# Reordering one turn of a woven attention pipeline: four steps change place in a hand-written order

## The chip, the cores and the metric

The kernel runs on one core of a Trainium2 chip. The metric is the device time of one launch in microseconds (us). Three executions of the kernel before took 490.29, 494.37 and 494.52 us, with a median of 494.37 us. A fourth one, the profiled execution, took 486.01 us.

## What is computed

Sixteen sequences of 256 rows and 128 columns go through three residual blocks. Everything is float32 at the interface.

```python
x = x + 0.5 * ffn(layernorm(x))      # gate, up, silu(gate)*up, down; inputs and weights rounded to FP4 in blocks of 16
x = x + attention(layernorm(x))      # 16 heads of 8, causal, softmax, output projection and bias
x = x + 0.5 * ffn(layernorm(x))
```

In the attention, scores are Q K^T / sqrt(8), masked below the diagonal, softmax over the keys, times V, then `Y @ Wo + bo`.

## The kernel before, in words

The kernel is written engine by engine: every engine has its own program, and semaphores tie them together. One batch is one sequence. The work on a batch is cut into named steps, and `ATT_LAG` says how many turns behind the newest batch a step works, so that in one turn each step works on another batch. A turn is one pass over `ATT_ORDER`. Each engine walks that same list and issues only its own part of each step, in the list's order. Inside an engine nothing overtakes: what stands behind a waiting instruction waits with it. So the list sets, for every engine at once, what is queued behind what.

Turns 0 to 4 of the attention are woven into the end of the first feed-forward block. Turns 5 to 7 run the full list, turns 8 to 15 are a loop of four turns, turns 16 to 19 again run the full list (with a few feed-forward steps between), and turns 20 to 22 use other lists. Turn 5 is the first with exponentials (ST0 to ST4), turn 7 the first with an output projection, turn 16 the last with a query-key projection. Turns 7 to 16 therefore hold both projections: ten turns. The norm's apply step ends with turn 16 too.

The steps that matter here, with their lines:

- `S0` to `S11`: TensorE computes scores (L1268), VectorE takes the row maximum of each (L1050). They use the PSUM banks s0, s1, s2 in turn.
- `nmS`: VectorE splits the maxima into three bf16 parts. `nm`: TensorE transposes them (L1278), ScalarE copies them out (L779, `nmT`), and a DMA issued by SyncE (L506) writes them into rows of `q_stack`.
- `ST0` to `ST11`: TensorE computes transposed scores, with the maxima subtracted through those rows (L1299), ScalarE takes the exponential (L790), GpSimd masks (L619). They use the banks st0 and st1 in turn, so TensorE's part of one waits for ScalarE's exponential of the one two before it. `ST0` also waits for the DMA of `nm`. In a turn the order is ST5 to ST11 of one batch, then ST0 to ST4 of the next.
- `AV0` to `AV3`: value products (L1326, L1330). `oc0`, `oc1`: ScalarE copies them out (L800). `oT0`, `oT1`: TensorE transposes them (L1341). `n0`, `n1`: VectorE divides by the row sums (L1073, L1075). `oT1` needs the bank that `n0` frees.
- `yT`: TensorE transposes the result (L1349). `yTc`: ScalarE copies it (L809). `wo`: TensorE's output projection (L1356), whose stationary operand is that copy. `wa`: VectorE adds it to x (L1083).
- `lnN`: ScalarE applies the norm to the next batch (L661). `xT`: TensorE transposes it (L1236). `xTc`: ScalarE copies it (L754). `qk`: TensorE's query and key projections (L1245). `c1`: ScalarE's first bf16 part of them (L760). `split`: VectorE's remainder (L1041). `c2`: the second part (L764).

Waits are placed by helpers such as this one of TensorE, which waits until the last user of the step's bank has been read:

```python
def bank_for(step, b, it):
    user = bank_user_before(step, it, NB)
    if user:
        k, n = count(*user)
        pe.wait_ge(taken[k], n)
...
def wo(b, s, it):
    ps, done = bank_for("wo", b, it)
    pe.wait_ge(taken["yT"], b + 1)
```

Of the kernel before, what the change touches and what calls it, by code (L numbers as in the profile page):

```python
# [82 lines left out]
    "oT0 oT1 n0 n1 yT yTc wo wa sS sA sE",  # L83
)) for step in steps.split()}
ATT_ORDER = """
nmS ST5 S0 oT0 third  ST6 lnN n0 S1  ST7 nm S2 stack  ST8 S3 AV0 AV1 bias
ST9 oc0 oT1 xT n1 S4  ST10 xTc lnS S5  ST11 lnA S6 yT  ST0 yTc lnE S7 qk wo
ST1 c1 wa S8  ST2 split S9 AV2 AV3  ST3 c2 oc1 sS S10 v  ST4 sA S11 sE
""".split()
ATT_UNROLL = 4  # L90
PART_TURNS = 2
# [1300 lines left out]
```

## Time and profile before

| what | value |
|---|---|
| profiled execution, device time | 486.01 us |
| span of its instructions | 484.3 us |
| outside the span | 1.7 us |
| TensorE matmul busy | 387.2 us (80%) |
| TensorE weight load busy | 283.9 us (59%) |
| VectorE busy | 425.9 us (88%) |
| ScalarE busy | 318.3 us (66%) |
| GpSimd busy | 258.1 us (53%) |
| mean granted TensorE clock | 0.979 of 2.4 GHz |
| median of three other executions | 494.37 us |

The busy shares are means over stages that differ. The first feed-forward block fills the span up to about 145 us, the attention with full turns runs from about 158 to 347 us, and the second feed-forward block ends at 484.3 us. The change touches only the middle part, so that part has to be read by itself, and there by the order in which waits end, since no engine's share alone says which one sets the pace. In the rows below, PE is TensorE, PEld its weight loads, DVE is VectorE, ACT is ScalarE, POOL is GpSimd.

### The profile page before, as it was taken

What the parts mean: (1) busy time and instruction counts of PE and PEld (TensorE: products, weight loads), DVE (VectorE), ACT (ScalarE), POOL (GpSimd) and SP (SyncE); (2) the same over time, 40 slices, a digit from 0 to 9 for tenths busy, and PEclk for the clock granted to TensorE, in tenths of its full rate; (3) what the DMA queues carried; (4) which work ended last, traced back from release to release, by engine and by line L of the source; (5) the groups of instructions that cost most, each with busy time, mean ns of one, the idle gap of its engine ahead of it and who ended that gap; (6) DMA issues with size and microseconds to landing.
All of it is one profiled execution on the core that took longest, in us unless ns stands there. A gap on an engine that the chain in (4) does not pass through costs nothing.

```text
span 484.3 us, 12396 instructions
## 1 busy us (share of the span) xinstructions
PE 387.2 (80%) x3433; PEld 283.9 (59%) x3433; DVE 425.9 (88%) x1132; ACT 318.3 (66%) x861; POOL 258.1 (53%) x479
## 2 busy tenths in 40 slices
PE   0557877878786799999999999988795777887786
PEld 0334656656574577777666767666553556665665
DVE  3787999998988989888888898888869989999994
ACT  3566788868752677777777787766763646656642
POOL 6464656645525466777777777555661243233321
PEclk9997999989999899999999999999998989999999
DMA  7887000000545454444445544450000000000001
GB/s 221 236 133 124 2 1 0 1 1 0 146 143 143 133 143 135 135 131 135 127 137 145 145 134 129 131 147 4 3 1 1 2 22 21 13 22 22 22 18 37
DMA packets 38440, 39.30 MB, mean 81 GB/s; under 512 B 1789, under 2 KB 35453, under 8 KB 36093
## 3 DMA queue, kind: packets, MB, share of 16 engines
q1 hardware_dynamic: 38397, 38.79, 30.3%
q8 instruction: 20, 0.33, 0.3%
q14 instruction: 23, 0.19, 0.1%
HBM read 21.91 MB, written 10.49 MB: 67 GB/s over the span
## 4 chain that ended last, share of the span: by engine, by line
PE 36%; issue 26%; ACT 11%; DVE 10%; POOL 8%; DMA 7%; ACTq 1%; POOLq 1%; SPq 0%; DVEq 0%
DMA q_stack<-nmT 6%; PE bank L1299 6%; PE bank L1326 5%; PE bank L1159 5%; PE bank L1160 4%; PE bank L1268 3%; ACT probs L790 3%; POOL hq_out L551 3%; PE bank L1188 2%; PE bank L1245 2%; PE bank L1356 2%; PE bank L1330 2%; POOL xq_out L551 2%; PE bank L1146 2%; POOL fln_rstd L577 1%
## 5 line engine op out<-in xcount | busy, mean ns | idle before, releaser
L790 ACT ACTIVATE probs<-bank 128x512 f32<-128x512 f32 x192 | 111.3, 603 | 48.3 <-PE bank L1299 47.2
L1050 DVE TENSOR_REDUCE nm<-bank 128x2 f32<-128x512 f32 (+1 forms) x192 | 125.9, 680 | 6.0 <-PE bank L1268 5.7
L619 POOL TENSOR_SCALAR_AFFINE_SELECT probs<-probs 128x256 f32<-128x256 f32 (+1 forms) x192 | 90.1, 485 | 62.5 <-ACT probs L790 61.0
L1299 PE MATMUL bank<-q_stack,k_stack 75*128 75x256 bf16 (+1 forms) x512 | 73.4, 247 | 9.9 <-ACT probs L790 5.5
L1268 PE MATMUL bank<-k_stack,q_stack 127*128 127x256 bf16 (+1 forms) x512 | 74.0, 249 | 1.5 <-DVE nm L1050 1.5
L551 POOL TENSOR_TENSOR xq_out<-xq_grid,xq_scale 128x256 f32<-128x256 bf16 x32 | 24.4, 762 | 83.5 <-DVE xq_grid L894 83.5
L1159 PE MATMUL bank<-wguT,f_xT 128*128 128x352 f32 x128 | 56.9, 529 | 6.7 <-ACT f_xT L713 4.5
L720 ACT ACTIVATE f_silu<-bank 128x352 f32<-128x352 f32 x64 | 29.6, 463 | 46.8 <-PE bank L1160 45.9
L1188 PE MATMUL bank<-wdT,f_hT 128*128 128x128 f32 (+1 forms) x384 | 53.4, 275 | 1.4 <-ACT f_hT L731 1.4
L1188 PEld LDWEIGHTS bank<-wdT,f_hT 128*128 128x128 f32 (+1 forms) x384 | 49.9, 191 | 6.5 <-issue 0.9
L1299 PEld LDWEIGHTS bank<-q_stack,k_stack 75*128 75x128 bf16 x512 | 37.1, 97 | 27.4 <-ACT probs L790 13.7
L1160 PE MATMUL bank<-wguT,f_xT 128*128 128x352 f32 x128 | 53.0, 499 | 0.0
L551 POOL TENSOR_TENSOR hq_out<-hq_grid,hq_scale 128x704 f32<-128x704 bf16 x31 | 42.8, 1380 | 11.7 <-DVE hq_grid L894 11.7
L1146 PE MATMUL bank<-ident,xq_out 128*128 128x128 f32 x64 | 14.2, 305 | 42.8 <-POOL xq_out L551 28.1
L1268 PEld LDWEIGHTS bank<-k_stack,q_stack 127*128 127x128 bf16 x512 | 40.8, 99 | 7.5 <-DVE nm L1050 3.1
L1326 PE MATMUL bank<-probs,v_stack 128*32 128x256 f32 x512 | 40.2, 386 | 0.2 <-DVE oT L1090 0.2
L1146 PEld LDWEIGHTS bank<-ident,xq_out 128*128 128x128 f32 x64 | 6.7, 144 | 51.2 <-POOL xq_out L551 31.8
L1015 DVE TENSOR_TENSOR f_h<-f_silu,bank 128x352 f32<-128x352 f32 x64 | 30.9, 515 | 6.4 <-ACT f_silu L720 6.1
L1160 PEld LDWEIGHTS bank<-wguT,f_xT 128*128 128x128 f32 x128 | 26.6, 208 | 15.9 <-issue 4.0
L1159 PEld LDWEIGHTS bank<-wguT,f_xT 128*128 128x128 f32 x128 | 23.3, 208 | 21.1 <-ACT f_xT L713 14.6
L1179 PE MATMUL bank<-ident,hq_out 128*128 128x128 f32 (+1 forms) x192 | 32.0, 276 | 4.0 <-ACT f_hT L731 3.6
L713 ACT COPY f_xT<-bank 128x256 f32<-128x256 f32 x31 | 11.5, 371 | 25.9 <-PE bank L1146 25.9
(149 smaller groups left out, 894.4 us busy)
## 6 DMA issues: line engine op xcount, KB each, us to landing
q_stack<-q_parts SPq DMA_DIRECT2D x16, 576.0 KB
k_stack<-k_parts SPq DMA_DIRECT2D x16, 576.0 KB
q_parts<-qk_parts SPq DMA_DIRECT2D x16, 192.0 KB, 2.1
k_parts<-qk_parts SPq DMA_DIRECT2D x16, 192.0 KB, 2.4
v_stack<-zeros_bf SPq DMA_DIRECT2D x1, 2048.0 KB, 10.2
k_parts<-qk_parts SPq DMA_DIRECT2D x16, 128.0 KB, 2.3
out_dram<-x_all SPq DMA_DIRECT2D x15, 128.0 KB, 1.8
q_stack<-mask_q SPq DMA_DIRECT2D x1, 1664.0 KB
```

The source lines that it names most:

```text
L551: nc.gpsimd.tensor_tensor(q.out[:, s, :].rearrange("p (n k) -> p n k", k=BLOCK), q.grid[:, s, :].rearrange("p (n k) -> p n k", k=BLOCK), q ...
L619: nc.gpsimd.affine_select(out=v, in_=v, compare_op=ALU.is_ge, fill=0.0, base=0, pattern=[[0, heads], [1, P]], channel_multiplier=-1).then_ ...
L790: nc.scalar.activation(probs[:, c, :], ps[:, :], ACT.Exp, scale=SCALE).then_inc(done, 1)
L1015: nc.vector.tensor_tensor(f_h[:, j, :], f_silu[:, j, :], ps.up[j][:, 0:I], ALU.mult).then_inc(h_ready[j], 1)
L1050: nc.vector.tensor_reduce(nm[:, j, h0:h0 + n], ps[:, :].rearrange("p (h k) -> p h k", h=n), AX_X, ALU.max, negate=True).then_inc(done, 1)
L1159: nc.tensor.matmul(ps.gate[j][:, 0:I], x, wguT[:, 0, :], start=True, stop=True)
L1160: nc.tensor.matmul(ps.up[j][:, 0:I], x, wguT[:, 1, :], start=True, stop=True).then_inc(gu_filled[j], 1)
L1179: last = nc.tensor.transpose(ps.hT[0:k, P * t:P * t + P], hquant.out[:, s, I * j + P * t:I * j + P * t + k], ident[:, :])
L1188: nc.tensor.matmul(out, f_hT[0:k, t, P * j:P * j + P], wdT[0:k, t, :], start=(t == 0), stop=False)
L1268: last = nc.tensor.matmul(ps[:, keys * h:keys * h + keys], q_stack[0:ROWS, s, h0 + h, P * j:P * j + P], k_stack[0:ROWS, s, h0 + h, 0:keys] ...
L1299: last = nc.tensor.matmul(ps[:, w * n:w * n + w], k_stack[0:SROWS, s, HG * g + h, k0:k0 + P], q_stack[0:SROWS, s, HG * g + h, q0:T], start ...
L1326: nc.tensor.matmul(ps[VW * h:VW * h + VW, 0:T], window(s, 0, h), probs[:, slot + h // 2, T * (h % 2):T * (h % 2) + T], start=(half == 0), ...
```

## The change

Only the list of one turn changes.

```diff
 ATT_ORDER = """
-nmS ST5 S0 oT0 third  ST6 lnN n0 S1  ST7 nm S2 stack  ST8 S3 AV0 AV1 bias
-ST9 oc0 oT1 xT n1 S4  ST10 xTc lnS S5  ST11 lnA S6 yT  ST0 yTc lnE S7 qk wo
-ST1 c1 wa S8  ST2 split S9 AV2 AV3  ST3 c2 oc1 sS S10 v  ST4 sA S11 sE
+nmS ST5 S0 oT0 third  ST6 n0 S1  ST7 nm lnN S2 stack  ST8 S3 oT1 n1 AV0 AV1 bias
+ST9 oc0 xT S4  ST10 xTc lnS S5  ST11 lnA S6 yT  ST0 yTc lnE S7 wo qk c1
+ST1 wa S8  ST2 split S9 AV2 AV3  ST3 c2 oc1 sS S10 v  ST4 sA S11 sE
 """.split()
```

No instruction is added or removed. VectorE, GpSimd and SyncE keep their orders: `n1` stays between S3 and S4 on VectorE, since the value products issue nothing there. TensorE and ScalarE change.

On TensorE, the end of a full turn's first half, before (S3 is the first row; L1326 and L1330 are AV0 and AV1, L1299 is ST9, L1341 is oT1, L1236 is xT):

```order
256 L1268 MATMUL bank<-k_stack,q_stack 128x128 x4
257 L1326 MATMUL bank<-probs,v_stack 32x256 x4
258 L1330 MATMUL bank<-probs,v_stack 32x128 x4
259 L1326 MATMUL bank<-probs,v_stack 32x256 x4
260 L1330 MATMUL bank<-probs,v_stack 32x128 x4
261 L1299 MATMUL bank<-q_stack,k_stack 128x256 x2
262 L1341 MATMUL bank<-ident,oT 128x128 x2
263 L1236 MATMUL bank<-ident,aln_out 128x128 x2
```

The same place now:

```order
256 L1268 MATMUL bank<-k_stack,q_stack 128x128 x4
257 L1341 MATMUL bank<-ident,oT 128x128 x2
258 L1326 MATMUL bank<-probs,v_stack 32x256 x4
259 L1330 MATMUL bank<-probs,v_stack 32x128 x4
260 L1326 MATMUL bank<-probs,v_stack 32x256 x4
261 L1330 MATMUL bank<-probs,v_stack 32x128 x4
262 L1299 MATMUL bank<-q_stack,k_stack 128x256 x2
263 L1236 MATMUL bank<-ident,aln_out 128x128 x2
```

The second output transpose has moved ahead of AV0, AV1 and ST9.

On TensorE, later in the same turn, before (the rows are yT, ST0, S7, qk, wo, ST1, S8):

```order
269 L1349 MATMUL bank<-ident,y 128x128 x2
270 L1299 MATMUL bank<-q_stack,k_stack 128x256 x2
271 L1268 MATMUL bank<-k_stack,q_stack 128x256 x2
272 L1245 MATMUL bank<-a_xT,wqk 128x256 x2
273 L1356 MATMUL bank<-wqkvo,yT 128x128 x2
274 L1299 MATMUL bank<-q_stack,k_stack 128x256 x2
275 L1268 MATMUL bank<-k_stack,q_stack 128x256 x2
```

The same place now:

```order
269 L1349 MATMUL bank<-ident,y 128x128 x2
270 L1299 MATMUL bank<-q_stack,k_stack 128x256 x2
271 L1268 MATMUL bank<-k_stack,q_stack 128x256 x2
272 L1356 MATMUL bank<-wqkvo,yT 128x128 x2
273 L1245 MATMUL bank<-a_xT,wqk 128x256 x2
274 L1299 MATMUL bank<-q_stack,k_stack 128x256 x2
275 L1268 MATMUL bank<-k_stack,q_stack 128x256 x2
```

The output projection and the query-key projection have changed places.

On ScalarE, a full turn from v's copy to c1, before (L790 are the exponentials: ST4 to ST6, then ST7, then ST8 and ST9, and so on):

```order
228 L772 COPY v_stack<-bank 128x32x8
229 L790 ACTIVATE probs<-bank 128x512 x3
230 L661 ACTIVATE aln_out<-x_all,aln_shift,aln_rstd 128x128 x2
231 L790 ACTIVATE probs<-bank 128x512
232 L779 COPY nmT<-bank 48x256
233 L790 ACTIVATE probs<-bank 128x512 x2
234 L800 COPY oT<-bank 128x256
235 L790 ACTIVATE probs<-bank 128x512
236 L754 COPY a_xT<-bank 128x256
237 L790 ACTIVATE probs<-bank 128x512 x2
238 L809 COPY yT<-bank 128x256
239 L790 ACTIVATE probs<-bank 128x512
```

The same place now:

```order
227 L772 COPY v_stack<-bank 128x32x8
228 L790 ACTIVATE probs<-bank 128x512 x4
229 L779 COPY nmT<-bank 48x256
230 L661 ACTIVATE aln_out<-x_all,aln_shift,aln_rstd 128x128 x2
231 L790 ACTIVATE probs<-bank 128x512 x2
232 L800 COPY oT<-bank 128x256
233 L790 ACTIVATE probs<-bank 128x512
234 L754 COPY a_xT<-bank 128x256
235 L790 ACTIVATE probs<-bank 128x512 x2
236 L809 COPY yT<-bank 128x256
237 L760 CAST qk_parts<-bank 128x512
```

The copy of the maxima now stands ahead of the norm, and the copy of queries and keys (L760) follows yTc directly, where the exponential of ST1 stood.

## Rows read from the trace of the kernel before

**Rows 1.** Busy time and granted clock in three stretches, all engines.

```profile
core 0: us, PE busy (x) PEld busy (x) DVE busy (x) ACT busy (x) POOL busy (x), PEclk, DMA share, GB/s
158.00:171.00 13.00, 10.15 (x102) 7.40 (x104) 12.39 (x26) 9.34 (x18) 6.08 (x13) 0.88 0.48 135
190.20:306.60 116.40, 109.40 (x1352) 81.38 (x1351) 102.40 (x284) 88.83 (x199) 83.11 (x177) 1.00 0.49 137
306.58:319.60 13.02, 11.09 (x146) 8.11 (x145) 10.58 (x28) 9.05 (x21) 7.70 (x16) 1.00 0.52 142
```

**Rows 2.** Waits of DVE from 195 to 345 us: total, times, longest.

```profile
DVE x_all L1083 <- PE bank L1356: 7.4, 12, 1.0
DVE row_inv L1073 <- PE bank L1341: 6.0, 12, 1.1
...
DVE qk_rest L1041 <- ACT qk_parts L760: 1.9, 9, 0.3
```

**Rows 3.** Chain that ended last, 260 to 300 us: start, length, what.

```profile
259.84 3.24 DMA q_stack<-nmT
...
289.41 0.87 PE bank L1245 x4
```

**Rows 4.** Timeline of ACT: start, length, instruction, [idle before <- releaser].

```profile
280.89 0.60 ACT L790 ACTIVATE probs<-bank 128x512 f32<-128x512 f32 x1 [0.85 <-PE bank L1299]
...
282.42 1.78 ACT L790 ACTIVATE probs<-bank 128x512 f32<-128x512 f32 x3
...
284.10 0.87 ACT L661 ACTIVATE aln_out<-x_all,aln_shift,aln_rstd 128x128 f32 x2
284.87 0.58 ACT L790 ACTIVATE probs<-bank 128x512 f32<-128x512 f32 x1
285.34 0.35 ACT L779 COPY nmT<-bank 48x256 bf16<-48x256 bf16 x1
...
286.77 0.60 ACT L790 ACTIVATE probs<-bank 128x512 f32<-128x512 f32 x1 [0.59 <-PE bank L1299]
...
287.65 0.60 ACT L790 ACTIVATE probs<-bank 128x512 f32<-128x512 f32 x1
...
288.40 0.62 ACT L790 ACTIVATE probs<-bank 128x512 f32<-128x512 f32 x1
289.31 0.60 ACT L790 ACTIVATE probs<-bank 128x512 f32<-128x512 f32 x1 [0.29 <-PE bank L1299]
289.80 0.37 ACT L809 COPY yT<-bank 128x256 f32<-128x256 f32 x1
...
293.68 0.60 ACT L790 ACTIVATE probs<-bank 128x512 f32<-128x512 f32 x1 [0.85 <-PE bank L1299]
```

**Rows 5.** Timeline of PE in the same turn.

```profile
283.10 0.39 PE L1299 MATMUL bank<-q_stack,k_stack 75*128 75x256 bf16 x2 [0.34 <-ACT probs L790]
...
286.35 0.39 PE L1299 MATMUL bank<-q_stack,k_stack 75*128 75x256 bf16 x2
286.57 0.38 PE L1341 MATMUL bank<-ident,oT 128*128 128x128 f32 x2
286.80 0.38 PE L1236 MATMUL bank<-ident,aln_out 128*128 128x128 f32 x2
...
288.80 0.39 PE L1299 MATMUL bank<-q_stack,k_stack 75*128 75x256 bf16 x2 [0.30 <-DMA q_stack<-nmT]
...
290.31 0.68 PE L1356 MATMUL bank<-wqkvo,yT 128*128 128x128 f32 x4
290.83 0.38 PE L1299 MATMUL bank<-q_stack,k_stack 75*128 75x256 bf16 x2
...
293.25 0.39 PE L1299 MATMUL bank<-q_stack,k_stack 75*128 75x256 bf16 x2
```

**Rows 6.** Timeline of PE in turn 18, which has no query-key projection.

```profile
327.37 0.38 PE L1268 MATMUL bank<-k_stack,q_stack 127*128 127x256 bf16 x2
328.57 0.68 PE L1356 MATMUL bank<-wqkvo,yT 128*128 128x128 f32 x4 [0.82 <-ACT yT L809]
```

## The prediction

> **What bounds the kernel now.** I read the busy time by stretches first. Over nine full turns VectorE is busy 102.40 of 116.40 us, TensorE 109.40 and ScalarE 88.83 [rows 1]. No engine is full, so something passes from engine to engine. The stretch gives an average turn of 116.40 / 9 = 12.93 us. Then I read VectorE's waits: in twelve turns it waits 7.4 us for the output projection, 6.0 us for the second output transpose and 1.9 us for the copy of queries and keys [rows 2]. These are just what three of the moved steps feed, so a first reading promises 15.3 us. But VectorE's waits count only if VectorE is on the chain that ends last. The chain answers that: in this part it runs through the DMA of the maxima, TensorE and ScalarE, and a query-key projection of 0.87 us stands on it [rows 3], while VectorE does not appear. The timelines of ScalarE and TensorE then let one turn be walked.
>
> **The turn before, walked.** Zero is the start of ST3's exponential at 280.89 us [rows 4]. ScalarE then works without a gap: ST4's exponential at 1.53, the norm at 3.21, ST7's at 3.98, the copy of the maxima at 4.45 [rows 4]. TensorE waits for the DMA and starts ST0 at 7.91 (288.80) [rows 5], 3.46 after the copy's start. ST0's exponential follows at 8.42 after a wait of 0.29, yTc at 8.91 [rows 4], wo at 9.42 and ST1 at 9.94 [rows 5]. ST3 starts at 12.36 [rows 5] and its exponential at 12.79 [rows 4]. So the cycle is copy, DMA, ST0, its exponential, yTc, wo, ST1 to ST3, exponentials, copy. The point is that TensorE runs the query-key projection between ST0 and wo, where wo waits for yTc anyway. A turn without that projection shows this: S7 starts at 327.37 and wo at 328.57, with TensorE idle 0.82 us for yTc, and what is queued behind does not fill it [rows 6].
>
> **Maxima copied ahead of the norm.** No instruction is added. The third of three exponentials starts at 282.42 + 2 x 0.59 = 283.60, the pitch being (1.78 - 0.60) / 2 [rows 4]. ST7's exponential can follow at 0.59, at 3.30, and the copy 0.47 later, at 3.77 instead of 4.45. With the same 3.46 the landing would allow ST0 at 7.23. The gain is between 0 and 0.68 per turn, as far as nothing else is late, and the next part is late. The norm ends near 4.9, and its reader xT starts at 5.91 [rows 5], so moving it back costs nothing. That cover is about 1 us.
>
> **Second transpose ahead of the value products.** It takes one issue place of 0.23 us (286.57 to 286.80) [rows 5] away from behind ST9 and puts it in front. ST9 starts at 5.46 + 0.22 = 5.68, xT where it was. ST9's exponential had waited 0.59 for TensorE [rows 4], so it moves from 5.88 to 6.10, and behind it ScalarE runs in a row to ST11's (287.65 and 288.40 become 6.98 and 7.73). ST0 needs the bank of ST10's exponential. From ST4's exponential to ST6's matmul, the same relation, it takes 283.10 - 282.42 = 0.68 [rows 4, 5], so ST0 starts at 7.66. Its exponential follows ST11's at 7.73 + 0.59 = 8.32, and this comes later than 7.66 + 0.51 = 8.17. So the two moves together give 0.10, not 0.68. VectorE's wait for this transpose goes (6.0 us in twelve turns), which buys nothing since VectorE then waits for wo. The transpose also waits for n0, which by the old timing is done just as S3 is issued. I take 0 for that and keep 0 to 0.3 for the range.
>
> **Output projection ahead of queries and keys.** yTc starts at 8.32 + 0.49 = 8.81 and wo at 9.32 (0.51 later, as before). TensorE has finished issuing S7 near 8.1, so it stands about 1.2 us, and everything else in its queue stands with it. Only then come the projection's 0.87 us [rows 3], which nothing hides any more. ST1 starts at 9.32 + 0.52 + 0.87 = 10.71 instead of 9.94. The bounds are 0, if yTc were ready when S7 is issued, and 0.87; the row of the turn without the projection says yTc is not ready, so I take 0.87. ST3 follows 2.42 later at 13.13, its exponential 0.43 later at 13.56.
>
> **The copy c1 ahead of ST1's exponential.** The projection's result is there near 10.9. ST1's exponential slips to about 11.4. ST3 needs that bank only 0.68 after, near 12.1, and comes at 13.13, so this costs 0. VectorE's 1.9 us of waits for the copy may go, but S8 now reaches VectorE later too, so I count no gain. If that cover of 1 us were gone, each turn would pay what is missing.
>
> **The sum.** A turn with both projections takes 13.56 instead of 12.93, or +0.63. Ten turns give +6.3 us. Turns 17 to 19 have neither the norm nor the query-key projection and keep only the earlier transpose, 3 x 0.22 = +0.7. In turn 5 there is no wo, and c1 no longer stands behind an exponential of 0.6, in front of a split that VectorE then waits for: between 0 and -0.6, I take -0.3. Together +6.7 us on an execution of 486.0 (span 484.3 and 1.7 around it), which makes 492.7. The median of the other executions is 8.4 us above the profiled one. Carried over unchanged, the sum gives 494.4 + 6.7 = 501.1, so 501. The forecast's own range is 498 to 503. About 1% is what a measurement of this kernel can tell from no change, and this is 1.4%.
>
> **Rival one, a longer landing (no measurable change).** The change gives the landing slack: ST0 may start as late as 8.32 - 0.51 = 7.81, or 4.04 after the copy, before it costs anything. Before, every tenth of it is paid each turn. In the chain it took 3.24 us from the DMA's issue to ST0 in one turn [rows 3], while the walked turn waited 0.30 for it, so it does vary. If half of the 8.4 us that ordinary executions take more lies there, 0.38 in each of eleven turns, the turn before is 13.31 and the turn after still 13.56: +2.5 for ten turns and +0.4 for the rest, 497.3 us. If all of it does, 0.76, then before it is 13.69. The landing of the average turn is 3.46 + (12.93 - 12.79) = 3.60, so after, ST0 comes at 3.77 + 3.60 + 0.76 = 8.13, 0.32 past the slack, so 13.88: +1.9 and +0.4, 496.7 us. For it speaks the spread of the executions, against it that nothing shows where the 8.4 us lie. The Trainium skill (DMA: Bandwidth & Descriptors, Latency and other measured facts) has the completion of a DMA depend on how loaded memory is; by that, a landing that differs between executions is plausible, and the sum would move toward this rival.
>
> **Rival two, VectorE sets the pace (faster).** If the chain's view were wrong and VectorE's waits were the price, the change would remove up to 7.4 + 6.0 + 1.9 = 15.3 us, which gives 479 us. It decides from the point where wo can start when S7 is issued, that is when yTc is ready by 8.1 instead of 9.3. Smaller gains on the same path end between 479 and 489. VectorE is busiest over the whole span, which speaks for it; the gap-free walk through ScalarE and TensorE speaks against.
>
> **Rival three, a late n0 (slower still).** If the transpose, now ahead of AV0, waits 0.3 for n0 in thirteen turns, all behind it slips: +3.9, 505 us.
>
> **The clock.** Granted clock was 1.00 (2.4 GHz) over the nine turns at a busy share of 109.40 / 116.40 = 0.94, and still 1.00 in turn 17 at 11.09 / 13.02 = 0.85; it was 0.88 over 158 to 171 us, where TensorE was busy 10.15 of 13.00 [rows 1]. After the change its share is about 12.2 / 13.56 = 0.90 (109.40 / 9 = 12.2 a turn), between those two, so I count no loss. The Trainium skill (TensorE: Matmul & The Clock Gate, HAM oscillation — how this bites in real kernels) warns that a wait inside every pass of a loop can drop the engine to half its clock each time. [...] As a mechanism here: at 1.2 GHz the TensorE parts of the walk (ST6 to ST9 3.5, wo, qk and ST1 to ST3 3.8) would double, 7 us a turn, far above any range. I give it 2 in 100.
>
> **How the numbers follow.** Forecast 0.53, rival one 0.29, rival two 0.08, rival three 0.08, the clock 0.02. Faster by over 1%: 0.08. Within 1%: rival one and little else, 0.30. Slower: 0.62. The range of 490 to 506 leaves out rival two's greater part, the clock and some of the tails.
>
> **What would show it.** In the changed profile, turns 7 to 16 should take about 13.5 us. TensorE should wait over 0.8 us for yT before L1356 in each of them. The wait for the DMA of the maxima should be gone, ST0 being released by ScalarE, and the copy of the maxima should directly follow ST7's exponential. VectorE should no longer wait for L1341; it should wait for scores (S8) about 0.8 us per turn instead. Turns 17 to 19 should be 0.2 us longer each. I am wrong if wo starts right behind S7, if the turn is under 12.9 us, or if VectorE has no waits left.

## The result and the profile after

The changed kernel takes 496.60 us (median of 16 runs, 494.59 to 500.03), the kernel before, run beside it, 490.34 us (16 runs, 487.49 to 496.22). The ratio is 1.0136, with a 95% interval of 1.0106 to 1.0165: slower by 1.4%, or 6.3 us. The sum had been +6.7 us on a base of 494.37. Ratios here and below leave out executions over 1.5% above the fastest of their kernel.

The profiled execution of the changed kernel has a span of 495.8 us, 11.5 more than before, so it exaggerates. Three stretches show where: the first and the last of them lie outside the nine turns that are compared below.

```profile
core 0: us, PE busy (x) PEld busy (x) DVE busy (x) ACT busy (x) POOL busy (x), PEclk, DMA share, GB/s
...
158.30:171.10 12.80, 10.35 (x68) 7.29 (x69) 10.85 (x24) 8.62 (x17) 6.44 (x13) 0.73 0.49 139
...
191.80:313.40 121.60, 109.63 (x1354) 80.52 (x1349) 103.25 (x283) 87.34 (x198) 83.13 (x177) 1.00 0.48 133
...
373.70:396.40 22.70, 15.11 (x48) 9.23 (x47) 19.60 (x58) 8.68 (x23) 5.26 (x7) 0.77 0.00 1
```

From 373.7 to 396.4 us the granted clock was 0.77, where the kernel before did the same steps in 19.9 us at 0.91: 2.8 us that no step of the change touches. Turn 5, at 158 us, ran at 0.73 and took 12.7 us between two copies of the maxima, against 11.2 before. The kernel before with half-size loads (below) took 12.9 there too, at 0.66, with its steps in the old order, while the changed kernel with one pair put back took 11.2 at 0.85. For the steps at 373.7, seven of the twelve kernels below take 19.9 to 20.2 us and five take 22.8 to 23.5, and the order of the engines does not sort them: the changed one is among the seven, that of before among the five. So these stretches vary between executions.

The nine turns in the middle do not suffer from it, at a clock of 1.00. From `wa` of turn 7 to `wa` of turn 16 (189.15 to 311.02 us) they take 121.87 us, 13.54 a turn. Before it was 187.58 to 303.94, 116.36 us, 12.93 a turn. That is +5.5 us in nine turns, against +5.7 by the sum. The tenth bare projection comes behind `wo` of turn 16, so it shows in the next distance, 13.96 us instead of 13.01. The two after that are 12.58 and 12.21 instead of 12.34 and 11.84. From `wa` of turn 7 to `wa` of turn 19 this makes +7.1 us, where ten turns and three transposes had been taken as +7.0.

VectorE's waits, 195 to 345 us, answer to [rows 2]:

```profile
DVE nm L1050 <- PE bank L1268: 14.0, 23, 0.9
DVE x_all L1083 <- PE bank L1356: 5.5, 11, 0.8
```

The waits for the transpose (6.0) and for c1 (1.9) are gone, that for wo fell from 7.4 to 5.5, and the waits for scores rose from 2.5 us to 14.0. In all VectorE waits 19.5 us where it waited 17.8. Its line for scores before:

```profile
DVE nm L1050 <- PE bank L1268: 2.5, 4, 0.7
```

TensorE's waits before, in the same stretch:

```profile
PE bank L1299 <- DMA q_stack<-nmT: 3.1, 7, 0.7
PE bank L1356 <- ACT yT L809: 2.5, 3, 0.8
```

TensorE's waits after:

```profile
PE bank L1356 <- ACT yT L809: 10.0, 11, 1.0
PE bank L1299 <- ACT probs L790: 4.7, 11, 1.0
PE bank L1299 <- DMA q_stack<-nmT: 0.6, 2, 0.4
```

It now stands 10.0 us in eleven turns for yTc instead of 2.5 in three, and the wait for the DMA of the maxima is down from 3.1 us to 0.6. One turn on ScalarE, to be laid beside [rows 4] (zero is ST3's exponential at 274.32):

```profile
274.32 0.60 ACT L790 ACTIVATE probs<-bank 128x512 f32<-128x512 f32 x1 [0.99 <-PE bank L1299]
...
278.00 0.36 ACT L779 COPY nmT<-bank 48x256 bf16<-48x256 bf16 x1
278.26 0.88 ACT L661 ACTIVATE aln_out<-x_all,aln_shift,aln_rstd 128x128 f32 x2
...
280.46 0.60 ACT L790 ACTIVATE probs<-bank 128x512 f32<-128x512 f32 x1 [0.84 <-PE bank L1299]
...
281.95 1.13 ACT L790 ACTIVATE probs<-bank 128x512 f32<-128x512 f32 x2
282.96 0.39 ACT L809 COPY yT<-bank 128x256 f32<-128x256 f32 x1
285.15 0.59 ACT L760 CAST qk_parts<-bank 128x512 bf16<-128x512 f32 x1 [1.80 <-PE bank L1245]
...
287.73 0.60 ACT L790 ACTIVATE probs<-bank 128x512 f32<-128x512 f32 x1 [0.99 <-PE bank L1299]
```

The same turn on TensorE, to be laid beside [rows 5, 6]:

```profile
278.24 0.42 PE L1341 MATMUL bank<-ident,oT 128*128 128x128 f32 x2
...
280.04 0.39 PE L1299 MATMUL bank<-q_stack,k_stack 75*128 75x256 bf16 x2
...
281.96 0.39 PE L1299 MATMUL bank<-q_stack,k_stack 75*128 75x256 bf16 x2
282.19 0.38 PE L1268 MATMUL bank<-k_stack,q_stack 127*128 127x256 bf16 x2
283.49 0.68 PE L1356 MATMUL bank<-wqkvo,yT 128*128 128x128 f32 x4 [0.92 <-ACT yT L809]
284.01 1.03 PE L1245 MATMUL bank<-a_xT,wqk 128*128 128x256 f32 x4
284.88 0.38 PE L1299 MATMUL bank<-q_stack,k_stack 75*128 75x256 bf16 x2
```

This is the picture of turn 18 before [rows 6], S7 and then a stand, but now with the whole query-key projection behind it. The steps of the sum, forecast and measured:

| place, us after ST3's exponential | before | forecast | after |
|---|---|---|---|
| copy of the maxima | 4.45 | 3.77 | 3.68 |
| ST9 on TensorE | 5.46 | 5.68 | 5.72 |
| ST9's exponential | 5.88 | 6.10 | 6.14 |
| ST0 on TensorE | 7.91 | 7.66 | 7.64 |
| yTc | 8.91 | 8.81 | 8.64 |
| wo | 9.42 | 9.32 | 9.17 |
| ST1 on TensorE | 9.94 | 10.71 | 10.56 |
| next exponential of ST3 | 12.79 | 13.56 | 13.41 |

### The profile page after: what moved, and what is told of

The parts are those of the page before. It is cut to its first block, busy times and chain, and to the rows that moved or that the text cites. A ratio compares the mean times of both kernels' runs of the same rounds, so it can differ in the third digit from the quotient of the medians.

```text
span 495.8 us, 12396 instructions
## 1 busy us (share of the span) xinstructions
PE 393.8 (79%) x3433; PEld 286.5 (58%) x3433; DVE 427.3 (86%) x1132; ACT 317.1 (64%) x861; POOL 257.9 (52%) x479
## 4 chain that ended last, share of the span: by engine, by line
PE 37%; issue 26%; ACT 11%; DVE 9%; POOL 8%; DMA 6%; SPq 1%; ACTq 1%; POOLq 1%; DVEq 0%
PE bank L1299 6%; PE bank L1326 6%; PE bank L1159 4%; PE bank L1268 4%; PE bank L1160 3%; DMA q_stack<-zeros_bf 3%; ACT probs L790 3%; POOL hq_out L551 3%; PE bank L1330 2%; PE bank L1356 2%; PE bank L1245 2%; PE bank L1188 2%; POOL xq_out L551 2%; POOL fln_rstd L577 2%; PE bank L1146 1%
## 5 line engine op out<-in xcount | busy, mean ns | idle before, releaser
L790 ACT ACTIVATE probs<-bank 128x512 f32<-128x512 f32 x192 | 108.4, 606 | 37.3 <-PE bank L1299 36.4
L1299 PE MATMUL bank<-q_stack,k_stack 75*128 75x256 bf16 (+1 forms) x512 | 74.3, 249 | 6.0 <-ACT probs L790 5.0
L1159 PE MATMUL bank<-wguT,f_xT 128*128 128x352 f32 x128 | 58.9, 545 | 6.1 <-ACT f_xT L713 4.0
L1160 PE MATMUL bank<-wguT,f_xT 128*128 128x352 f32 x128 | 54.0, 506 | 0.0
L1299 PEld LDWEIGHTS bank<-q_stack,k_stack 75*128 75x128 bf16 x512 | 36.9, 98 | 26.1 <-ACT probs L790 11.7
L1326 PE MATMUL bank<-probs,v_stack 128*32 128x256 f32 x512 | 40.2, 386 | 0.2 <-DVE oT L1090 0.2
L1160 PEld LDWEIGHTS bank<-wguT,f_xT 128*128 128x128 f32 x128 | 27.3, 213 | 16.7 <-issue 5.4
L1159 PEld LDWEIGHTS bank<-wguT,f_xT 128*128 128x128 f32 x128 | 24.1, 214 | 21.1 <-ACT f_xT L713 14.1
L713 ACT COPY f_xT<-bank 128x256 f32<-128x256 f32 x31 | 11.6, 373 | 26.9 <-PE bank L1146 26.9
```

The source lines that it names most:

```text
L790: nc.scalar.activation(probs[:, c, :], ps[:, :], ACT.Exp, scale=SCALE).then_inc(done, 1)
L1159: nc.tensor.matmul(ps.gate[j][:, 0:I], x, wguT[:, 0, :], start=True, stop=True)
L1160: nc.tensor.matmul(ps.up[j][:, 0:I], x, wguT[:, 1, :], start=True, stop=True).then_inc(gu_filled[j], 1)
L1299: last = nc.tensor.matmul(ps[:, w * n:w * n + w], k_stack[0:SROWS, s, HG * g + h, k0:k0 + P], q_stack[0:SROWS, s, HG * g + h, q0:T], start ...
L1326: nc.tensor.matmul(ps[VW * h:VW * h + VW, 0:T], window(s, 0, h), probs[:, slot + h // 2, T * (h % 2):T * (h % 2) + T], start=(half == 0), ...
```

## The experiments

Twelve kernels were run. The turns below are differences of `wa`'s start (L1083) on VectorE in each one's profile; "nine turns" are those from turn 7 to turn 16, 116.36 us in the kernel before. Ratios are to the kernel before, timed beside it.

### The parts alone

Theory one: the bare query-key projection is the price. Theory two: VectorE's waits are. First the changed kernel with one pair put back:

```diff
-ST9 oc0 xT S4  ST10 xTc lnS S5  ST11 lnA S6 yT  ST0 yTc lnE S7 wo qk c1
+ST9 oc0 xT S4  ST10 xTc lnS S5  ST11 lnA S6 yT  ST0 yTc lnE S7 qk wo c1
```

> The changed kernel with one pair put back: queries and keys ahead of the output projection on TensorE; the other three moves stay. Theory one (the bare query-key projection is the price): ST1 starts at 9.84 instead of 10.71 after ST3's exponential, the turn is 12.7 us, nine such turns 114.3, and the kernel is 2 us faster than before (ratio 0.996, between 0.990 and 1.000). TensorE's wait for yT before L1356 falls under 0.3 us a turn. Theory two (VectorE's waits are the price): VectorE has no waits for the transpose and the copy, so 7.9 us less than before, ratio 0.984. Theory three (the earlier transpose delays all): still slower than before by 2 us or more.

Measured: 1.0011 (0.9978 to 1.0044). The price is gone with this pair, as theory one has it. VectorE has lost its waits for the transpose and for c1 and the kernel gains nothing, so theory two falls. But it is not faster than before either: nine turns took 115.9 us instead of 114.3, among them single ones of 12.6, about as forecast, and others of 13.3 and 13.7. TensorE still waits for the DMA of the maxima, 2.3 us in three of the turns.

Then the kernel before with only that pair exchanged:

```diff
-ST9 oc0 oT1 xT n1 S4  ST10 xTc lnS S5  ST11 lnA S6 yT  ST0 yTc lnE S7 qk wo
+ST9 oc0 oT1 xT n1 S4  ST10 xTc lnS S5  ST11 lnA S6 yT  ST0 yTc lnE S7 wo qk
```

> The kernel before with only the output projection put ahead of queries and keys. Theory one: ST0 stays bound by the DMA at 7.9 to 8.05, wo at 9.4 to 9.6, then the projection's 0.87 us bare: the turn is 13.7 to 13.8 us, nine turns 124, and the kernel is 8 us slower than before (ratio 1.016, between 1.012 and 1.020), more than the whole change. Theory two: VectorE's wait for wo falls, so it is faster or the same.

Measured: 1.0104 (1.0064 to 1.0143), nine turns in 121.2 us. This one exchange has nearly the whole effect. It is smaller than I expected, though: most turns take 13.4 to 13.5 us, not 13.7 to 13.8. I had added the projection to a landing of 3.5 us, and the waits of TensorE say the landing is no longer waited for:

```profile
PE bank L1356 <- ACT yT L809: 9.7, 11, 0.9
...
PE bank L1299 <- DMA q_stack<-nmT: 0.4, 2, 0.3
```

The copy of the maxima stands behind the norm here as before, at 4.45. So the landing itself must have become shorter. In the turn around 280 us SyncE issues the DMA at 280.44 and ST0 starts at 283.16, 2.72 later, where the walked turn before took 2.94.

Only the maxima ahead of the norm:

```diff
-nmS ST5 S0 oT0 third  ST6 lnN n0 S1  ST7 nm S2 stack  ST8 S3 AV0 AV1 bias
+nmS ST5 S0 oT0 third  ST6 n0 S1  ST7 nm lnN S2 stack  ST8 S3 AV0 AV1 bias
```

> The kernel before with only the copy of the maxima ahead of the norm. Theory one: with the transpose where it was, ST9 stays at 5.46, ST0 starts at 7.45, its exponential at 8.10 to 8.15 instead of 8.42 (8.56 on the average turn), so the turn is 12.5 us, nine turns 112.5, and the kernel is 4.5 us faster than before (ratio 0.991, between 0.986 and 0.996). TensorE's wait for the DMA of the maxima is gone. Theory two: VectorE's three waits are untouched, so no change.

Measured: 1.0002 (0.9968 to 1.0036), nine turns in 117.3 us. Theory one misses by 4.5 us. The wait for the DMA, which I said would be gone, is 5.7 us in eight turns, with a longest of 1.3 us. The turns go 12.50, 12.65, 13.55, 12.66, 12.88, 13.60, 13.08, 13.78, 12.59: some as forecast, some a whole microsecond longer.

Only the transpose ahead of the value products:

```diff
-nmS ST5 S0 oT0 third  ST6 lnN n0 S1  ST7 nm S2 stack  ST8 S3 AV0 AV1 bias
-ST9 oc0 oT1 xT n1 S4  ST10 xTc lnS S5  ST11 lnA S6 yT  ST0 yTc lnE S7 qk wo
+nmS ST5 S0 oT0 third  ST6 lnN n0 S1  ST7 nm S2 stack  ST8 S3 oT1 n1 AV0 AV1 bias
+ST9 oc0 xT S4  ST10 xTc lnS S5  ST11 lnA S6 yT  ST0 yTc lnE S7 qk wo
```

> The kernel before with only the second output transpose (and its division) ahead of the value products. Theory one: ST9 starts 0.22 us later, but ST0 still waits for the DMA, so turns 7 to 16 stay at 12.9 us and turns 17 to 19 get 0.2 us longer each: +0.7 us (ratio 1.001, between 0.997 and 1.005). VectorE's wait for L1341 falls from 6 us in twelve turns to under 1. Theory two: those 6 us are gained, ratio 0.988.

Measured: 1.0016 (0.9981 to 1.0050), nine turns in 117.3 us. VectorE's 6.0 us for L1341 are gone and nothing is gained. Turns 17 to 19 took 13.09, 12.57 and 12.23 us, against 12.86, 12.35 and 11.84 in runs with the old place and no waits for the DMA: +0.23, +0.22 and +0.39, where the sum has 0.22 each.

### What the landing of the maxima waits for

Two runs missed in the same place, the landing that I had taken as a fixed 3.46 us. SyncE's queue of the kernel before, in the walked turn (L506 is the DMA of the maxima, L488 the stores of the next batch's parts, L496 the loads that fill the score stacks):

```profile
278.90 0.82 SPq L496 DMA_DIRECT2D q_stack<-q_parts  x1
279.77 0.79 SPq L496 DMA_DIRECT2D k_stack<-k_parts  x1
...
285.86 0.74 SPq L506 DMA_DIRECT2D q_stack<-nmT  x1
288.27 0.38 SPq L488 DMA_DIRECT2D q_parts<-qk_parts  x1
...
291.72 0.83 SPq L496 DMA_DIRECT2D q_stack<-q_parts  x1
```

The DMA engines' share in three stretches around it (next to last column):

```profile
283.00:285.86 2.86, 2.77 (x46) 2.03 (x50) 2.76 (x8) 2.79 (x8) 2.49 (x6) 1.00 0.73 189
285.86:287.00 1.14, 1.14 (x22) 0.84 (x15) 0.68 (x3) 0.55 (x2) 1.14 (x3) 1.00 0.33 86
287.00:288.80 1.80, 1.50 (x16) 1.16 (x15) 1.77 (x6) 1.78 (x5) 1.80 (x4) 1.00 0.05 14
```

When the maxima are issued, the two loads of 576 KB each are still moving, until about 287. And the stores of the next batch are issued at 288.27, though GpSimd's third part (L604, 285.38 + 1.17) was ready at 286.55: SyncE's step `stack` first waits for the previous loads. That is a loop of its own: stores to loads 291.72 - 288.27 = 3.45, loads to the stores that wait for their landing 288.27 - 278.90 = 9.37, together 12.8 us, which is the walked turn. Between 190 and 305 us SyncE waits 11.6 + 1.8 us in the kernel before for the last of each batch's loads. In the run with the maxima ahead, the same views of one of its long turns read:

```profile
274.24 0.74 SPq L506 DMA_DIRECT2D q_stack<-nmT  x1
277.89 0.38 SPq L488 DMA_DIRECT2D q_parts<-qk_parts  x1
```

```profile
271.20:274.20 3.00, 2.66 (x35) 1.87 (x36) 2.86 (x10) 2.93 (x8) 1.69 (x6) 1.00 0.80 210
274.24:276.00 1.76, 1.76 (x37) 1.23 (x30) 1.45 (x3) 1.17 (x4) 1.76 (x3) 1.00 0.49 127
276.00:278.20 2.20, 1.66 (x18) 1.31 (x15) 2.02 (x6) 2.15 (x5) 2.20 (x6) 1.00 0.07 14
```

```profile
278.24 0.39 PE L1299 MATMUL bank<-q_stack,k_stack 75*128 75x256 bf16 x2 [0.59 <-DMA q_stack<-nmT]
```

ScalarE started the copy 3.68 us after ST3's exponential (273.72 and 270.04), 0.77 earlier than before, and the DMA was issued at 274.24. But TensorE's ST0 starts 4.00 us after the issue instead of 2.94, at 8.20 after ST3's exponential and so later than the 7.91 before. What was gained on ScalarE is given back in the DMA. The new theory: the loads bound the kernel before, the engine chain of yTc, wo and ST3 being about as long. Its rival was my old view of a fixed landing. To tell them apart, the loads were cut to half from the fifth batch on; such a kernel leaves out half of the data that the scores need, and serves for timing alone:

```diff
-                    turns = bass.AP(parts.tensor, parts.offset, [[H * T, PARTS * D], [apart, PARTS], [1, H * T]])
-                    sp.dma_start(stack[0:QROWS, s], turns).then_inc(stacks_loaded, 16)
+                    n = H if first(b, ATT_UNROLL) else H // 2
+                    turns = bass.AP(parts.tensor, parts.offset, [[H * T, PARTS * D], [apart, PARTS], [1, n * T]])
+                    sp.dma_start(stack[0:QROWS, s, 0:n], turns).then_inc(stacks_loaded, 16)
```

On the kernel before:

> The kernel before, in which the two loads that fill the score stacks bring only heads 0 to 7 from the fifth batch on; heads 8 to 15 keep the data of earlier batches. New theory (the loads bound the kernel before: the copy of the maxima lands behind them, and SyncE's stores of the next batch wait for them, a loop of 12.9 us by itself): with half the data the loop opens, ST0 no longer waits for the DMA, the turn is 12.5 us, nine turns 112.5, and the kernel is 4 to 5 us faster than before (ratio 0.991). Old theory (the landing takes a fixed 3.5 us after the copy): turns stay at 12.9 us, ratio 1.000.

Measured: 0.9859 (0.9823 to 0.9895), nine turns in 113.4 us, most of them 12.54 to 12.70. TensorE's wait for the DMA is 0.5 us in twelve turns, the order of the engines being untouched (the edit adds a line, so L1300 is L1299 of the other kernels, and so on).

```profile
PE bank L1300 <- ACT probs L791: 4.7, 11, 1.0
PE bank L1357 <- ACT yT L810: 2.5, 3, 0.8
PE bank L1300 <- DMA q_stack<-nmT: 0.5, 2, 0.3
```

With the maxima ahead of the norm, and the same half loads:

> Half loads as in the run above, and the copy of the maxima ahead of the norm. New theory: ST0 is bound by TensorE's queue and the exponential of ST10 in both, so the same 12.5 us a turn as with half loads alone, ratio 0.991, and the turns no longer vary between 12.5 and 13.8. Old theory: 12.5 us here and 12.9 with half loads alone, a difference of 4 us or more.

Measured: 0.9934 (0.9895 to 0.9973). The profile has nine turns in 111.9 us, seven of them 12.39 to 12.53, so the long ones are gone and the turn is 0.17 us shorter than with half loads alone. The median, 488.9 against 485.9 us, goes the other way, while the spans of the profiles are 484.0 and 484.8. The granted clock, averaged over an execution, goes with it: three of the twelve executions here had 0.965 to 0.968 and took 484.9 to 485.7 us, the other nine had 0.951 to 0.954 and took 488.6 to 490.8. All six with half loads alone had 0.963 to 0.968. At a like clock the two kernels are level within 0.5 us.

On the changed kernel, the same half loads:

> The changed kernel with half loads (heads 8 to 15 keep the data of earlier batches from the fifth batch on). New theory: the chain through wo and the bare query-key projection sets the turn, not the loads, so the regular turns stay at 13.4 us and only the long ones (13.8) shrink to it: nine turns 120.5 to 121, ratio to the kernel before 1.011 to 1.013, and 9 us above the kernel before with half loads. Rival (the loads bind both kernels): it falls by 4 us or more, like the kernel before.

Measured: 1.0075 (1.0045 to 1.0106), under the range I gave. The turns are nearly as expected: 121.3 us for nine, six of them 13.41 or 13.42, one of 13.30, and two of 13.78. Those two are turns 8 and 12, where the loop of four turns starts over; they come back in the other runs, so they are not the loads. Against the changed kernel with full loads that is 0.6 us less in nine turns, and the kernel before gains 2.9 us from the same cut: the two are bound by different things.

### The stores ahead of the wait for the loads

The loop can be opened with everything computed. The wait for the previous loads is moved from ahead of the stores to ahead of the loads:

```diff
                 wait_apart(sp, parts3_ready, b + 1, passed_sp)
-                if not first(b, 1):
-                    wait_apart(sp, stacks_loaded, 16 * N_LOADED * b, passed_sp)
...
                 wait_apart(sp, parts_stored, 16 * N_STORED * (b + 1), passed_sp)
+                if not first(b, 1):
+                    wait_apart(sp, stacks_loaded, 16 * N_LOADED * b, passed_sp)
```

> A version that computes everything: the kernel before with the copy of the maxima ahead of the norm, and in SyncE's step stack the wait for the previous batch's loads moved from ahead of the stores to ahead of the loads. New theory: the stores are issued 1.7 us earlier, as soon as the third part is ready, the loads follow that much earlier and are landed before the maxima need the way, so the turn is 12.5 us and the kernel is 4 us faster than before (ratio 0.992, between 0.987 and 0.998). If the loads' own 9 us and not the order of waits sets the loop, or if stores and loads slow each other, the turn stays at 12.9 us or above.

Measured: 0.9855 (0.9814 to 0.9896), better than the range. Nine turns take 112.0 us, most of them 12.39 to 12.52, the 12.5 that had been expected of the maxima's copy alone. TensorE's wait for the DMA of the maxima and SyncE's wait for the previous loads (11.6 + 1.8 us before) are gone. SyncE's queue shows the stores issued right behind the third part, which ends at 271.39 + 1.16 = 272.55, and the loads 12.40 us after the previous ones:

```profile
263.78 0.83 SPq L496 DMA_DIRECT2D q_stack<-q_parts  x1
...
271.10 0.73 SPq L506 DMA_DIRECT2D q_stack<-nmT  x1
272.65 0.37 SPq L486 DMA_DIRECT2D q_parts<-qk_parts  x1
...
276.18 0.84 SPq L496 DMA_DIRECT2D q_stack<-q_parts  x1
```

That edit alone, with the engines' order of before:

> The kernel before with nothing changed but SyncE's wait for the loads, put behind the stores. Theory: the landing of the maxima shortens to 2.7 us from its issue, as with half loads, and the turn to 12.55 to 12.6 us: nine turns 113.3, ratio 0.992 (0.987 to 0.997). The copy of the maxima ahead of the norm is then worth the remaining 0.15 to 0.2 us a turn, where by itself it was worth nothing.

Measured: 0.9838 (0.9788 to 0.9887), below the range; nine turns in 113.65 us, 113.3 expected. One of its six executions took 765.75 us; nothing on record says why, and it is left out of the ratio. The copy of the maxima ahead of the norm is then worth 113.65 - 112.00 = 1.65 us in nine turns, 0.18 each. By itself it was worth nothing.

The changed kernel with the same edit:

> The changed kernel with the stores ahead of the wait for the loads, all computed. Theory (bare query-key projection sets the turn in the changed kernel, the loads do not): turns 13.4 us, nine turns 121, ratio to the kernel before 1.010, and about 11 us above the version with the maxima's copy and the stores ahead but the old order of the rest (0.86 by the projection and 0.22 by the transpose in each of ten turns). Rival (the loads bind the changed kernel too): it falls to the time of the kernel before or under it.

Measured: 1.0052 (1.0023 to 1.0081). Nine turns take 121.3 us, 13.40 or 13.41 each but for the loop's starts (13.77) and the last (13.30). TensorE's wait for yTc is what it was:

```profile
PE bank L1356 <- ACT yT L809: 10.0, 11, 1.0
```

The difference to the run of the same edit with the maxima ahead is 121.29 - 112.00 = 9.3 us in nine turns, 1.03 each, where 0.86 for the projection and 0.22 for the transpose make 1.08. This is what the rest of the change costs once the loads are out of the way. The ratio is again under the expected one although the turns fit; that is taken up below.

Of the change's other parts, c1 ahead of ST1's exponential, on top of maxima and stores ahead:

```diff
-ST9 oc0 oT1 xT n1 S4  ST10 xTc lnS S5  ST11 lnA S6 yT  ST0 yTc lnE S7 qk wo
-ST1 c1 wa S8  ST2 split S9 AV2 AV3  ST3 c2 oc1 sS S10 v  ST4 sA S11 sE
+ST9 oc0 oT1 xT n1 S4  ST10 xTc lnS S5  ST11 lnA S6 yT  ST0 yTc lnE S7 qk wo c1
+ST1 wa S8  ST2 split S9 AV2 AV3  ST3 c2 oc1 sS S10 v  ST4 sA S11 sE
```

> The maxima's copy ahead of the norm, stores ahead of the wait for the loads, and of the change's other parts only the copy c1 ahead of ST1's exponential. Theory: it stands on no chain, 12.4 us a turn, nine turns 112, the same time as without it within 0.3% (ratio to the kernel before 0.986); VectorE's wait for c1 falls from 1.9 us to under 1.

Measured: 0.9841 (0.9796 to 0.9886), nine turns in 112.4 against 112.0 us. VectorE's wait for c1 is gone, and it buys nothing.

Last, a version aimed at what the walk leaves: yTc stands behind ST0's exponential on ScalarE. It is moved ahead, on top of the maxima and the stores ahead:

```diff
-ST9 oc0 oT1 xT n1 S4  ST10 xTc lnS S5  ST11 lnA S6 yT  ST0 yTc lnE S7 qk wo
+ST9 oc0 oT1 xT n1 S4  ST10 xTc lnS S5  ST11 lnA S6 yT yTc  ST0 lnE S7 qk wo
```

> A version that computes everything: copy of the maxima ahead of the norm, stores ahead of the wait for the loads, and yTc now also ahead of ST0 in the list, so that ScalarE copies y before ST0's exponential. With the loads out of the way the chain through yTc and wo sets the turn: yTc starts at 8.0 to 8.1 after ST3's exponential instead of 8.5, wo at 8.8 behind the query-key projection's own end instead of 9.0, ST0's exponential 0.25 later without harm. The turn is 12.2 us instead of 12.4, nine turns 110.1, and the kernel is 2 us under the version without this move (ratio to the kernel before 0.981). Rival: ST0's later exponential delays ST2's and so ST3: no gain.

Measured: 0.9794 (0.9743 to 0.9846), a median of 482.70 us (6 runs, 479.03 to 487.97), 11.2 us under the kernel before beside it. Nine turns take 109.5 us, and turns 17 to 19 take 12.40, 11.75 and 11.25 instead of 12.86, 12.35 and 11.84. It computes everything, and it is faster than both kernels. The rival of a later ST0 falls with that.

## Why the prediction was right, and where not

**The result.** Slower by 6.3 us where the sum said 6.7, and 496.6 us where it said 501. Nearly all of the second difference is the base: the kernel before has a median of 490.34 over 16 runs, not the 494.37 of three. Read alone, the 496.6 would have been rival one's 496.7; only the difference to the kernel beside it decides for the sum.

**The subtraction: part luck.** The walk had the turn go from 12.79 to 13.56, +0.77, but the sum took 13.56 less the average turn of 12.93, +0.63. The walked turn after is 13.41, and the average one 13.54. So the walk ended 0.15 late, and the sum left out that the average turn after would stand above its walk too, by 0.13. The two errors cancel, and the average turn grew by 0.61, close to the 0.63.

**Output projection ahead of queries and keys: right.** I took 0.87 us of bare projection per turn. In the walked turn wo to ST1 went from 0.52 to 1.39, just that. The exchange alone gives 1.0104, the changed kernel without it is level with before (1.0011), and VectorE's freed waits gave nothing in either of the two kernels that had them freed without the exchange, nor in the one with c1 ahead. From S7 to wo it is 283.49 - 282.19 = 1.30 between starts, 0.92 of it idle.

**The second transpose: right.** ST9 came 0.26 later, where 0.22 had been taken, and turns 17 to 19 took 0.23, 0.22 and 0.39 more with this move alone. The last of them is more than a place in the queue; why was not tried.

**c1: right.** With the stores ahead it gave 112.4 us in nine turns against 112.0 without, no gain. The -0.3 us that I took for it in turn 5 can't be seen: that turn takes 11.2 to 12.9 us in the profiles, whatever the order.

**The maxima ahead of the norm: wrong.** The step that failed is "With the same 3.46 the landing would allow ST0 at 7.23". The landing is no constant. It comes after the loads in whose tail the maxima are issued, and issued earlier it took longer by more than was gained (4.00 us instead of 2.94 from issue to ST0, with the copy 0.77 earlier). The kernel with this move alone missed its expectation by 4.5 us. In the sum the error hid, because I had let the transpose eat the gain down to 0.10 in any case, and because after the change TensorE seldom waits for this DMA (0.6 us in two turns). That is luck: without the transpose in front, the sum would have counted a gain that is not there.

**What bounds the kernel before: half right.** The gap-free walk is true, and so was the denial of VectorE. But two loops of about the same length ran side by side: the one through yTc and wo, and SyncE's from stores to loads to stores, 3.45 + 9.37 us. Opening the second alone shortened the average turn by 0.30 us (113.65 against 116.36 us in nine turns). The chain of waits named the DMA of the maxima, and I stopped there and did not ask what that DMA stood behind. The average turn of 12.93, from which I took the difference, was set by the loads, and so the base of the subtraction was right by measurement and not by my mechanism.

**Rival one, a longer landing:** half of it holds. The changed kernel is nearly insensitive to the loads and their landing, and the kernel before is not. But the spread of the executions, which spoke for this rival, goes with the granted clock, averaged over an execution, and it does so where no landing is waited for. Of the sixteen executions of the changed kernel four had 0.959 and took 499.8 to 500.0 us, and four had 0.972 to 0.974 and took 494.6 to 496.0. The kernel with half loads and the maxima ahead, whose TensorE does not wait for this DMA, spread by 6 us in the same way. The profiled execution of the kernel before, with its 486.01 us, had 0.979, and the 72 later ones of that kernel had 0.948 to 0.976. So a part of the 8.4 us probably goes with the clock; how much was not measured. What the prediction cites here from the Trainium skill (DMA: Bandwidth & Descriptors, Latency and other measured facts) is said there of load on HBM. This DMA goes from one tile in SBUF to another, so no run here bears it out.

**The ratios that missed while the turns fit.** The clock accounts for them in part. Beside the kernels with half loads the kernel before had a median clock of 0.959, and they had 0.967 (the kernel before with half loads) and 0.969 (the changed one). Taking only executions at 0.965 to 0.969, the medians are 489.7 us before (6), 485.3 with half loads (5) and 496.0 for the changed kernel with half loads (8). That is 0.991 and 1.013, the ratios expected. Beside the changed kernel with the stores ahead only three executions of the kernel before had such a clock, from 488.2 to 494.2 us, too few to say. Why one kernel's executions get a higher clock than another's was not isolated.

**Rivals two and three:** the faster one is refuted by the result and by the four kernels of "The parts alone". A late n0 did not show: S3 starts at 278.02, the transpose at 278.24, AV0 at 278.60, and ST9 comes 0.04 later than forecast.

**The clock:** it was 1.00 over the nine turns at a busy share of 109.63 / 121.60 = 0.90 and a stand of 0.9 us in each. The case that the Trainium skill warns of (TensorE: Matmul & The Clock Gate, HAM oscillation — how this bites in real kernels) is a loop whose wait for a DMA is longer than the matmuls of a pass; a stand of 0.9 us in a turn of 13.5 is not that case, and the prediction read the warning too widely. The clock fell elsewhere, to 0.73 in turn 5 and 0.77 at 373.7 us, and the kernel before has its dips at the same places, 0.87 and 0.91.

## What to carry to other kernels

When a step waits for the last link of a chain (here yTc), work that is ready belongs ahead of it in an in-order queue, even if the longest wait of another engine is for the step that waits (here VectorE's 7.4 us for wo). A wait that a profile puts down to a small DMA is a question and not an answer: look at what the same DMA engines carry when it is issued, and whether the queue that issues it waits for something it needn't. And where two loops have about the same length, shortening the shorter one shows nothing until the other is opened: the copy of the maxima was worth nothing alone and 0.18 us a turn once the loads were out of the way, which alone gave 0.30. Last, two kernels that are compared by a few executions should be compared by their granted clocks too.

## What the runs showed of the hardware that I had not expected

A DMA of 24 KB took 2.94 us from issue to the start of the matmul it releases when it was issued 1.1 us before the loads ahead of it ran out (DMA share 0.33 until then), and 4.00 us when it was issued 1.8 us before their end (0.49). In both cases the matmul started about 2 us after the share had fallen to 0.05 or 0.07. Over more turns: issued 5.5 to 6.3 us behind the loads, as in turns of the kernel with only the maxima ahead, it took 3.6 to 4.7 us; 6.5 to 7.4 us behind them, in the kernel before, 2.8 to 3.4; and 7.7 to 8.3 us behind them, with half loads, 2.7 to 2.9. Where TensorE did not wait for the DMA these are upper bounds. The Trainium skill (DMA: Bandwidth & Descriptors, Queues, rings and completion order) says each DMA engine takes the descriptors of a ring in order. The trace does not contradict that, and does not show it: whether order in the ring or shared bandwidth is the cause was not told apart.

The granted clock, averaged over an execution, differs between executions of one kernel, and the time with it: 0.959 and 500.0 us, 0.972 and 494.6 us for the changed kernel. In all fourteen profiles, with 0.955 to 0.979 over the whole, the nine turns had 1.00, so in them the clock was lost outside the nine turns.
